# Block 0's attention sums as identity products on TensorE, normalisation 3 on ScalarE, and the shared expert's first products on four banks

## Time and profile before

| | |
|---|---|
| runs | 1786.31, 1786.4, 1788.27 us, median 1786.4 |
| the profiled execution's own time | 1787.39 us |
| its span, first to last instruction | 1785.3 us |
| TensorE's mean granted clock | 0.977 of 2.4 GHz |
| first half | to about 1165 us |
| busy TensorE, VectorE, ScalarE, GpSimd | 1662.2, 1212.4, 805.2, 1190.9 us |

### The profile page before, as it was taken

How to read it: one execution, slowest core, us unless ns; L and a number is a source line. 1 busy time by engine, 2 the same in 40 slices (tenths; PEclk the granted TensorE clock), 3 DMA queues, 4 the chain that set the end, 5 groups by cost and what they waited for, 6 DMA issues and landing times.

```text
span 1785.3 us, 25208 instructions
## 1 busy us (share of the span) xinstructions
PE 1662.2 (93%) x7115; PEld 1203.4 (67%) x7161; DVE 1212.4 (68%) x2117; ACT 805.2 (45%) x1837; POOL 1190.9 (67%) x668
## 2 busy tenths in 40 slices
PE   2588999999999999999999998989999999999997
PEld 1354665665665665566566565668888888888886
DVE  7999999999999999999999996132222222222221
ACT  4255556556565465465465454323232323223232
POOL 4978889899898898898898893224333333433333
PEclk8798999999999999999999999989999999999999
DMA  5102112111111112112112112066777767777774
GB/s 201 47 13 71 48 40 57 48 34 50 59 29 53 56 27 59 47 35 59 48 35 60 48 25 60 25 188 158 156 166 154 169 152 166 157 157 164 155 169 77
DMA packets 89455, 157.19 MB, mean 88 GB/s; under 512 B 8896, under 2 KB 72128, under 8 KB 89024
## 3 DMA queue, kind: packets, MB, share of 16 engines
q1 hardware_dynamic: 60512, 112.58, 20.4%
q0 software_dynamic: 28896, 44.06, 14.6%
HBM read 101.79 MB, written 48.56 MB: 84 GB/s over the span
## 4 chain that ended last, share of the span: by engine, by line
PE 56%; DVE 20%; POOL 12%; issue 8%; ACT 3%; DMA 1%; POOLq 0%; SPq 0%; DVEq 0%; ACTq 0%
PE p_b L1502 10%; PE p_b L1513 10%; PE p_q L1502 7%; PE p_b L1332 7%; PE p_b L1379 6%; PE p_b L1445 5%; DVE p_q L931 5%; POOL prod_pool L496 4%; DVE prod L922 4%; DVE prod L945 4%; PE p_v L1502 3%; POOL prod_pool L510 2%; DVE qkv L958 2%; PE p_q L1304 2%; POOL prod_pool L517 2%
## 5 line engine op out<-in xcount | busy, mean ns | idle before, releaser
L611 POOL DMA_INDIRECT out_rows<-prod_pool,prod x142 | 220.7, 1554 | 383.6 <-ACT prod_pool L849 353.3
L496 POOL TENSOR_TENSOR prod_pool<-prod_pool 128x2048 f32<-128x2048 f32 (+2 forms) x192 | 370.7, 1931 | 15.1
L1379 PE MATMUL p_b<-bT,fc_sb 128*128 128x512 f32 x512 | 230.4, 604 | 1.3 <-ACT bT L781 1.3
L1332 PE MATMUL p_b<-proj_sb,hid 128*128 128x256 f32 x1024 | 230.5, 379 | 0.0
L1332 PEld LDWEIGHTS p_b<-proj_sb,hid 128*128 128x128 f32 x1024 | 189.6, 190 | 29.4 <-issue 0.5
L931 DVE TENSOR_REDUCE p_q<-prod 128x128 f32<-128x2048 f32 (+1 forms) x64 | 189.3, 2957 | 1.2
L922 DVE TENSOR_TENSOR prod<-p_q,eqk 128x4096 f32<-128x4096 f32 (+1 forms) x48 | 186.8, 3891 | 4.8 <-DVE attn L971 0.3
L945 DVE TENSOR_TENSOR prod<-p_q,v_dve 128x4096 f32<-128x4096 f32 (+1 forms) x48 | 186.8, 3891 | 1.6
L958 DVE TENSOR_REDUCE qkv<-prod 128x256 f32<-128x4096 f32 (+1 forms) x48 | 186.6, 3887 | 1.6
L1502 PE MATMUL p_b<-prod,exp_up 128*128 128x256 f32 x840 | 187.1, 379 | 0.0
L1445 PE MATMUL p_b<-x3T,sgup_sb 128*128 128x512 f32 x384 | 177.5, 601 | 6.4 <-issue 5.5
(11 more groups left out here) (179 smaller groups left out, 2880.7 us busy)
## 6 DMA issues: line engine op xcount, KB each, us to landing
exp_up<-in_experts SPq DMA_DIRECT2D x71, 768.0 KB
prod<-rows_sorted SPq DMA_DIRECT2D x71, 260.0 KB
xin<-in_x SPq DMA_DIRECT2D x16, 512.0 KB, 3.4
xres<-in_x SPq DMA_DIRECT2D x16, 512.0 KB, 3.7
xres<-xmid POOLq DMA_DIRECT2D x16, 512.0 KB, 4.6
out_rows<-x SPq DMA_DIRECT2D x16, 512.0 KB, 2.9
exp_dn<-in_experts SPq DMA_DIRECT2D x8, 384.0 KB, 5.1
out_rows<-prod_pool,prod POOLq DMA_INDIRECT x142, 3.8
```

Source lines behind the costliest of these rows:

```text
L496: done(g.tensor_tensor(prod_pool[:, at:at + n * w], prod_pool[:, at:at + n * w], prod_pool[:, at + n * w:at + 2 * n * w], ALU.add))
L611: pool.indirect_dma_start(out=out[:, :], out_offset=bass.IndirectOffsetOnAxis(ap=tok_i[j][:, a:a + 1], axis=0), in_=yg[j][:, a * D:(a + 1) ...
L1332: ins = t_.matmul(o, src[:, k, t * P:(t + 1) * P], w[:, k, :], start=k == 0, stop=bias_at is None and k == chunks - 1)
L1379: ins = t_.matmul(bnk[:], fc_sb[:, k, f * P:(f + 1) * P], bT[:, k, :], start=k == 0, stop=k == KC - 1)
```

## The change

1. **Block 0** has lists of its own on four engines (`first_block`). VectorE and GpSimd make the products; the sums over 16 terms are 16 products with the identity that accumulate in PSUM, on TensorE (`sums_of`); ScalarE copies GpSimd's scores back (`take_sums`). Products lie in `prod`, `hid`, `prod_pool` and in the space of the expert weights, whose loads therefore wait for block 0's attention.
2. **Biases** are split in two parts: Q, K, V ahead of the first features, the rest in block 0. Constants follow there, and so the spare rows' stores, which move to round 1. The first statistics are taken by VectorE; tiles are normalised in the order of use, and a transpose waits for its tile alone.
3. **Normalisation 3** goes to ScalarE, by sums and squares in two halves (`ln3_scales`), ahead of the copy of tile 1. `products_2` of tile 3 is cut in halves, with the second addition between them.
4. **Shared first products on four banks**: b2, b3, b0, b1, b2, b3; two, not one, stand ahead of part P of tile 1.
5. **Token numbers** are advanced by ScalarE, not GpSimd.
6. **Between the halves**: ranks after two of four `down` tiles, the last gate product in three pieces, expert weights requested ahead of the rows, first expert product ahead of the second tile's transposes.

```diff
+        bias_left, bias_part = (z[:].rearrange("p k n -> p (k n)")[:, lo:lo + 5 * D] for z, lo in ((sg_g, 0), (sg_u, D)))
...
+        own_2, share_n = (HEADS - POOL_HEADS) * HH, POOL_HEADS * HH
+        first_at = (None, prod, spare[:, 0:own_2], hid[:].rearrange("p f n -> p (f n)"))
+        first_share = spare[:, own_2:own_2 + share_n]
+        first_v = sg_u[:, 0, 0:D].rearrange("p (e g) -> p e g", e=HD)
...
-        shared_bank = (p_b2, p_b3, p_b0, p_b2, p_b3, p_b2)
+        shared_bank = (p_b2, p_b3, p_b0, p_b1, p_b2, p_b3)
...
                 if isinstance(c, int) and c in (1, 2):
+                    sp.wait_ge(attn_ready, 1)
                     for e in range((c - 1) * EXPERTS // 2, c * EXPERTS // 2):
                         sp.dma_start(exp_dn[:, e, :], experts[e, :, EXU:EXW]).then_inc(experts_in, 16)
+                if isinstance(c, int) and c == 1:
+                    store_spares()
...
             sp.wait_ge(tables_ready, 1)
+            load_up(0, 0)
+            load_up(1, 1)
             sp.wait_ge(pads_stored, 16 * EXPERTS)
             sp.wait_ge(scattered, 16 * 2 * TPB * BLOCKS)
...
             load(0, 0)
-            load_up(0, 0)
             load(1, 1)
-            load_up(1, 1)
...
             def scatter(c, j):
+                wait(pool, tok_written, c - 1)
                 wait(pool, slots_ready, c - 1)
-                stand_alone(pool)
-                done(g.tensor_scalar(tok[:], tok[:], float(BLOCK), None, ALU.add))
-                stand_alone(pool)
-                done(g.tensor_copy(rows[j % 2][:, :, C_TOK], tok[:]))
...
-            def scales_3(c):
-                wait(act, x1_read, c)
-                a.activation(sq_c[:], mv_c[:, :, 1], ACT.Ln, bias=eps_1[:, 0:1]).then_inc(ln3_log, 1)
-                act.wait_ge(ln3_log, c)
+            def ln3_scales(c, j, k):
+                tiles = range(TPB // 2 * k, TPB // 2 * (k + 1))
+                half, n = slice(tiles[0], tiles[-1] + 1), 2 * (c - 1) + k + 1
+                wait(act, x1_read, n)
+                for t in tiles:
+                    a.activation(act_junk[:, t, :], x1[(j + 1) % 2][:, t, :], ACT.Copy, accum_out=sum_c[:, t:t + 1]
+                                 ).then_inc(ln3_sum, 1)
+                act.wait_ge(ln3_sum, TPB // 2 * n)
+                a.activation(mean_c[:, half], sum_c[:, half], ACT.Copy, scale=-1.0 / D).then_inc(ln3_mean, 1)
+                act.wait_ge(ln3_mean, n)
+                for t in tiles:
+                    a.activation(act_junk[:, t, :], x1[(j + 1) % 2][:, t, :], ACT.Square, bias=mean_c[:, t:t + 1],
+                                 accum_out=square_c[:, t:t + 1]).then_inc(ln3_var, 1)
+                act.wait_ge(ln3_var, TPB // 2 * n)
+                a.activation(sq_c[:, half], square_c[:, half], ACT.Ln, bias=eps_1[:, 0:1], scale=1.0 / D
+                             ).then_inc(ln3_log, 1)
+                act.wait_ge(ln3_log, n)
                 wait(act, rows_ready, TPB * (c - 1))
-                a.activation(rs_c[:, 0, :], sq_c[:], ACT.Exp, scale=-0.5).then_inc(ln3_std, 1)
+                a.activation(rs_c[:, 0, half], sq_c[:, half], ACT.Exp, scale=-0.5).then_inc(ln3_std, 1)
+                act.wait_ge(ln3_std, n)
+                for t in tiles:
+                    a.activation(rs_c[:, 1, t:t + 1], rs_c[:, 0, t:t + 1], ACT.Copy, scale=mean_c[:, t:t + 1]
+                                 ).then_inc(ln3_scale, 1)
...
+            def token_numbers(c, j):
+                a.activation(tok[:], tok[:], ACT.Identity, bias=block_1[:, 0:1]).then_inc(tok_moved, 1)
+                act.wait_ge(tok_moved, c - 1)
+                a.activation(rows[j % 2][:, :, C_TOK], tok[:], ACT.Copy).then_inc(tok_written, 1)
+            def take_sums(i, lo, n):
+                act.wait_ge(first_pool, i + 1)
+                a.activation(s_pool[:, lo:lo + n, :].rearrange("p h g -> p (h g)"),
+                             p_b3[:, lo * HEADS:(lo + n) * HEADS], ACT.Copy).then_inc(s_taken, 1)
...
+                if stage_c:
+                    token_numbers(c, j)
...
+                first = isinstance(c, int) and c == 0
+                if first:
+                    take_sums(0, 0, HEADS)
                 if more:
                     ln1_scales(c + 1)
                     norm_1(c + 1)
+                if first:
+                    take_sums(1, HEADS, POOL_HEADS)
+                if more:
                     take_x(c + 1, 0)
                     take_x(c + 1, 1)
                     take_qkv(c + 1, 0)
+                if stage_b and (more or not core):
+                    ln3_scales(c, j, 0)
+                    ln3_scales(c, j, 1)
+                if more:
                     take_qkv(c + 1, 1)
-                if stage_b:
-                    scales_3(c)
...
+                if core and not more:
+                    table_exp_ln()
+                    ln3_scales(c, j, 0)
+                    ln3_scales(c, j, 1)
...
             table_exp_ln()
-            for i in range(2 * TPB):
-                ln1_sums(0, i)
+            act.wait_ge(ln1_mean, 1)
             ln1_scales(0)
             norm_1(0)
...
+                for u in (1, 2, 3):
+                    features(0, u)
+                    done.sync()
+                    announce(dve, products_qk(u, first_at[u]), first_p, u)
+                    if u < 3:
+                        dve.sem_inc(pq_free, 1)
+                for u in (1, 2, 3):
+                    n = own_heads(u)
+                    wait(dve, first_s, u)
+                    s = bank[u][:, 0:width[u]].rearrange("p (h g) -> p h g", h=n)
+                    done(v.tensor_reduce(den_first[:, at[u]:at[u] + n], s, AX.X, ALU.add))
+                    if u == 3:
+                        wait(dve, s_taken, 2)
+                        done(v.tensor_reduce(den_first[:, at[4]:], s_pool[:], AX.X, ALU.add))
+                        done(v.tensor_scalar(den_first, den_first, 1e-6, None, ALU.add))
+                        done(v.reciprocal(inv_first[:], den_first))
+                    v_u = first_v if u == 1 else v_dve[u % 2][:]
+                    announce(dve, v.tensor_tensor(
+                        first_at[u][:, 0:n * HH].rearrange("p (h e g) -> p h e g", h=n, e=HD),
+                        s.unsqueeze(2).to_broadcast([P, n, HD, HEADS]),
+                        v_u.unsqueeze(1).to_broadcast([P, n, HD, HEADS]), ALU.mult), first_p, 3 + u)
+                dve.sem_inc(pq_free, 1)
+                wait(dve, pool_qk_used, 1)
+                features(1, 0)
+                dve.wait_ge(feat_ready, 5)
+                bias_rows(3 * D, 5 * D)
+                constants()
...
@@ -997,20 +1136,8 @@
                     wait(dve, rows_ready, TPB * (c - 2))
                 flat, res = (z[:].rearrange("p t d -> p (t d)") for z in (x1_b, xres))
                 wait(dve, proj_psum, 2 * (c - 1) + k + 1)
-                done(v.tensor_tensor(flat[:, 512 * k:512 * k + 512],
...
-            def shift_3(c):
...
+                v.tensor_tensor(flat[:, 512 * k:512 * k + 512], res[:, 512 * k:512 * k + 512], (p_b0, p_b1)[k][:],
+                                ALU.add).then_inc(x1_read, 1)
...
                 if core:
                     wait(dve, pool_s, c + 1)
                     done.later(v.tensor_reduce(total[:, HEADS:], s_pool[:], AX.X, ALU.add))
-                    products_2(c, 3, True)
+                    products_2(c, 3, False, 0, half)
                 if stage_b:
                     residual_2(c, j, 1)
                 if core:
+                    products_2(c, 3, True, half, HEADS)
                     if more:
                         wait(dve, pool_qk_used, c + 1)
                         features(c + 1, 0)
...
-                if stage_b:
-                    shift_3(c)
...
+            wait(dve, xin_loaded, 16)
+            stats(lambda t: xin[:, t, :], mv_first)
+            v.tensor_scalar(mean_a[:], mv_first[:, :, 0], -1.0, None, ALU.mult).then_inc(ln1_mean, 1)
+            v.tensor_scalar(square_a[:], mv_first[:, :, 1], float(D), None, ALU.mult).then_inc(ln1_var, TPB)
+            dve.sem_inc(ln1_sum, TPB)
...
+                announce(dve, ins, bias_ready, 1 if lo == 0 else 2)
+            def constants():
...
+            dve.wait_ge(weights_in[0], 16 * 7)
+            dve.wait_ge(pool_const, 6)
+            done(v.memset(bias_bf[:], 0.0))
+            done(v.tensor_scalar(bias_left[:, 0:2 * D], bias_left[:, 0:2 * D], 1.0, None, ALU.add))
+            bias_rows(0, 3 * D)
             features(0, 0)
...
             def gate_last():
-                wait(dve, up_taken, 2 * HCH * BLOCKS)
                 wait(dve, shared_h, BLOCKS - 1)
-                announce(dve, v.tensor_tensor(sg_g[:], sg_g[:], sg_u[:], ALU.mult), shared_h, BLOCKS)
+                for i in range(HCH):
+                    wait(dve, up_taken, 2 * HCH * (BLOCKS - 1) + 2 * (i + 1))
+                    ins = v.tensor_tensor(sg_g[:, i, :], sg_g[:, i, :], sg_u[:, i, :], ALU.mult)
```

(65 more changed lines are left out.)

181 lines of the change are left out of this document (113 added, 68 removed).

## The result

The changed kernel takes **1813.8 us** (median of 4 runs, 1813.5 to 1814.4), the kernel before 1787.2 beside it: a ratio of 1.0149, 95% interval 1.0131 to 1.0166. It is 1.5% slower. The forecast was 1771.9, range 1763 to 1795. It was wrong in sign and in size, by 42 us, and rival 2, "the strided reads are slow", had said 1808.

A forecast was written before the change was run, and what follows sets the result against it. Steady block: TensorE, VectorE and GpSimd nearly full, period 18 us of TensorE's list plus 50 of VectorE's. 16.2, down to 13.6, - 22.8 + 0.6 - 5.9 = -14.5: 1787.39 to 1772.9, as median 1771.9; range 1763 to 1795.

The forecast's parts named there:

- rival 2: First block: strided reads twice as slow, 36.4 us in two phases, total 1808; decides from 14.5 us, 1.4 times; chance 0.17.
- The first block: Block 0: sums on TensorE, 96 wide records at 0.216, 28.5 us a phase, next features at 96.7, +16.2 us.
- A rule against it: First block's identity sums: a skill note says reads crossing 16-byte lines pay; no row shows TensorE's; by it, rival 2's sum.
- Narrow records: First block's identity sums: 64 narrow records a phase between 6.9 and 12.2 us, taken as 7.7.
- Order of block 0: Block 0: first L922 at 23.7, sums from 31.2, 4.4 us between the phases, sums continuous on TensorE.
- Rival 4: First block: some sums at TensorE's lower clock, each idle us bringing one at half speed, +5 to +12; chance 0.13.
- Rival 1: First block: identity products cost one record, a phase 14 us, features at about 63, total 1739; chance 0.07.
- Blocks 1 and 2: Block 1 loses VectorE's 1.61 wait before L985, attention ends at +15; block 2 gains 1.7, block 3's projection at +13.6.
- The steady block: Attention blocks 3 to 15: period 68.2 to 66.3, gain 1.9, twelve periods -22.8; L985 with no wait.
- Rival 3: Each block: ScalarE's statistics come late and hold eqk, by the 1.9 gained, total 1794.7; chance 0.08.
- The last attention block and the seam: Last attention block: statistics ahead of ScalarE's transpose copy, +0.6; seam: first expert product at 1182.5, not 1189.0, in all -5.9.
- Weights are requested ahead of it: Seam: expert weights are requested ahead of the scatter's last part, which comes at 1175.6 instead of 1179.99.

The follow-up runs named there:

- e1: The changed kernel with VectorE writing its six first-block products in the order that TensorE reads: 1782.2 us, 0.9972 of the kernel before.
- e6: The changed kernel with its old first block, except tile 1's sums on TensorE, strided, and the biases' second part ahead of the first products: 1785.8 us.
- e9: e6 with e7's load order, bias casts made by ScalarE into PSUM and constants ahead of the first features: 1751.9 us, 0.9805 of the kernel before.
- e4: The changed kernel with one, not two, of the shared expert's first products ahead of the next Q/K/V: 1835.0 us, 1.0265 of the kernel before.
- e7: The changed kernel with its old first block, and tile 1's expert weights requested after the sorted rows: 1765.5 us, against 1768.5 without the latter.
- e11: e9 with the transposes of the expert half's second tile ahead of the first expert products again: 1751.9 us, 0.9799 of the kernel before.

## Why the prediction was wrong, point by point

**The step that failed** is in "The first block": "16 in 3.62 ... so 0.216 each", applied to the 96 wide records of a phase. It held for the third of them that read GpSimd's tile (0.216). The 64 that read VectorE's tiles took 0.431, the 32 strided narrow ones 0.271. So a phase is 64 x 0.431 + 32 x 0.216 + 32 x 0.271 + 32 x 0.111 = 46.7, the chain's 46.76, and two phases are 36.5 us over the forecast. Rival 2 had the mechanism, the records and the price (36.4), at a chance of 0.17. The text's own rule for where it decides (14.5 us, 1.4 times) was right; what was wrong was the weight. I had the step in the code, a VectorE row with 1.4 times (0.58 against 0.41) as the nearest, and the note quoted in "A rule against it": three signs for, and none against but that no row of TensorE showed it. e1 takes the step away and has 28.6 for the 28.5.

**Narrow records:** 7.7 taken, 32 x (0.136 + 0.111) = 7.9 in e1. Right.

**Order of block 0:** start at 23.7 (23.1), sums from 31.2 (30.9), 4.4 between the phases (4.5), no gap within: right. Rival 4 did not come: the granted clock was 1.00 in both phases. Its price, one us at half speed for each us idle, is no rule either: after 3.99 us idle the clock was 0.50 for the next 3.0 us at least (e1), after 32.04 us idle for only some 4 (e6). After 0.99 us idle it stayed at 1.00 in the changed kernel (78.80 to 80.00) and was 0.53 in e9 (45.80 to 49.40), so the length of the idle time alone does not tell it. Rival 1 neither: 32 records for 16 products.

**Blocks 1 and 2:** the step "In block 1 VectorE's wait of 1.61 before L985 goes" was a misreading, and this account of it rests on VectorE's timeline. Before and after, what the chain calls "issue" there (1.61 us from 86.31, 1.96 from 138.37) lies inside VectorE's own sum:

```profile
85.72 2.29 DVE L931 TENSOR_REDUCE p_q<-prod 128x128 f32<-128x2048 f32 x1
87.93 1.27 DVE L985 TENSOR_TENSOR xmid<-xmid,p_b 128x512 f32<-128x512 f32 x2
```

```profile
138.12 2.29 DVE L1021 TENSOR_REDUCE p_q<-prod 128x128 f32<-128x2048 f32 x1
140.32 1.27 DVE L1124 TENSOR_TENSOR xmid<-xmid,p_b 128x512 f32<-128x512 f32 x2
```

There was no wait that could go. The addition and TensorE's projection kept their distance to the block's start, VectorE still idled 2.65 us ahead of the second addition (2.6 forecast), and block 1 lost 0.3 us where 1.2 were to be gained. Block 2 gained 2.6 where 1.4 were forecast. Together they gave 2.3 instead of 2.6, which is luck: two misses that cancel. A piece called "issue" in a chain does not show an idle engine; the engine's timeline does.

**The steady block:** 65.9 us (forecast 66.3), by the reason given, as e4 shows. The sentence that L985 would not wait was wrong: it waits 1.4 in the mean of 13 blocks (L1124 now), since TensorE's own sum, 65.3 of 65.9, is now the bound, which the same paragraph had named as near. Rival 3 did not come.

**The last attention block and the seam:** the attention ends +22.6, the copies for TensorE +25.4, its projection +28.5. The forecast's 13.6 - 22.8 + 0.6 is -8.6 and, with the 36.2 of the first block, +27.6. It is right to 0.9 by luck: it took the gain of thirteen attentions (27.5) as twelve (22.8), and the loss behind the last one as 0.6 instead of 5.9. ScalarE's statistics stand ahead of its copy, TensorE idles 5.92 us for it, and then runs at half speed, four records here against the same four before:

```profile
1122.74 2.04 PE L1475 MATMUL p_b<-wo_sb,bT 128*128 128x256 f32 x4 [5.92 <-ACT bT L750]
```

```profile
1097.34 1.10 PE L1332 MATMUL p_b<-wo_sb,bT 128*128 128x256 f32 x4 [0.67 <-ACT bT L706]
```

Of the 5.9, 2.8 are the late copy; the rest are records at the lower clock (0.56 granted from 1122.70 to 1126.00, 0.66 from 1131.00 to 1135.50; 1.00 before). The term that was left out is this clock. At the seam 3.5 of 6.5 came up to the first expert product. "Weights are requested ahead of it" was counted as harmless; e7 measures it at 3. Behind the first expert product another 1.5 went, 0.6 forecast: TensorE does the second tile's transposes there and waits 0.78 us for ScalarE's copy; e11 puts at most 0.9 of it to the order.

## What to carry to other kernels

Before work moves to another engine, ask in what order that engine will read what the first one wrote: for TensorE 4-byte elements more than 8 bytes apart cost up to double here (the table above). If a step in the access can't be removed, put it on the engine that is idle there, in this kernel TensorE for one tile of the first block (1751.9) and not for all (1813.8). When no row shows a doubtful access and a named mechanism says that it is slow, that is no small rival. An engine that has to wait can cost more than the wait: after 4 to 6 us idle TensorE's next records ran at half speed (e1, the last attention block).
